# Expert blocks with both weight halves in one matmul, biases moved into the mixing, GRU state split shared with GpSimd

## The reference

```python
def step(h, xz):                              # 196 steps, h is (16, 192)
    h_z, h_r, h_n = jnp.split(h @ Wh.T + bh, 3, axis=-1)
    z = jax.nn.sigmoid(x_z + h_z)
    r = jax.nn.sigmoid(x_r + h_r)
    ncand = jnp.tanh(x_n + r * h_n)
    h_new = (1.0 - z) * ncand + z * h
...
top_v, top_i = jax.lax.top_k(softmax(xf @ gate_w.T), 2)     # the two best of 8, weights made to sum to 1
for e in range(8):
    w_e = jnp.sum(jnp.where(top_i == e, top_v, 0.0), axis=-1)
    y = _gelu(xf @ fc1_w[e].T + fc1_b[e]) @ fc2_w[e].T + fc2_b[e]      # 192 -> 512 -> 192
    out = out + w_e[:, None] * y
shared = _gelu(xf @ w1_w.T + w1_b) * (xf @ w3_w.T + w3_b) @ w2_w.T + w2_b
```

## Time and profile before

| | |
|---|---|
| median of 3 runs | 1919.51 us (1915.17 to 1924.06) |
| the profiled execution | 1919.37 us, span 1917.6 us |
| busy | PE 1503.1 (78%), PEld 1286.0 (67%), DVE 1313.1 (68%), ACT 951.3 (50%), POOL 740.5 (39%) |
| mean granted TensorE clock | 0.788 |
| GRU steps | 103.9 to 530.6 us of the span, PE 83% busy, clock 0.50 |
| expert blocks | 1241 to 1446 us, PE 100% busy, clock 0.99 |
| mixing | 1453 to 1486 us, PE 39% busy, clock 0.50 |

### The profile page before, as it was taken

The page is one execution under the profiler, slowest core; times in us unless marked ns, Lnnn a source line. Parts: engine busy times, 40 slices in busy tenths (PEclk is TensorE's granted clock), DMA queues, the critical chain, the costliest instruction groups (busy, mean ns, idle before and its releaser), DMA issues. The chain is left out here.

```text
span 1917.6 us, 51586 instructions
## 1 busy us (share of the span) xinstructions
PE 1503.1 (78%) x19477; PEld 1286.0 (67%) x19477; DVE 1313.1 (68%) x4844; ACT 951.3 (50%) x1918; POOL 740.5 (39%) x675
## 2 busy tenths in 40 slices
PE   4778888888845878889756899599994288888887
PEld 4667777777734867767544677388883277676766
DVE  7788888888857478778646674344444655787874
ACT  3633333333335577778614234344442256787881
POOL 3700000000022167779733012345550405686994
PEclk9955555555576999999885579799996589999998
DMA  2000000000032686668142204312224358676832
GB/s 82 4 4 4 4 4 4 4 4 4 4 106 87 164 232 147 147 126 148 26 127 74 90 25 162 117 57 66 63 63 147 103 156 225 140 165 127 161 59 58
DMA packets 62671, 167.20 MB, mean 87 GB/s; under 512 B 16648, under 2 KB 40184, under 8 KB 59740
## 3 DMA queue, kind: packets, MB, share of 16 engines
q1 hardware_dynamic: 57052, 151.05, 31.6%
q0 software_dynamic: 5376, 12.85, 2.3%
HBM read 95.84 MB, written 67.42 MB: 85 GB/s over the span
## 5 line engine op out<-in xcount | busy, mean ns | idle before, releaser
L903 POOL TENSOR_TENSOR l_arena<-l_arena,l_arena 98x784 fp32r<-98x784 f32 x192 | 354.7, 1860 | 110.0 <-PE l_ps L1012 72.5
L434 PE MATMUL gru_ps_r<-gru_hp,gru_wp 128*128 128x16 f16 x3920 | 200.5, 176 | 70.3 <-DVE gru_hp L406 69.5
L434 PEld LDWEIGHTS gru_ps_r<-gru_hp,gru_wp 128*128 128x128 f16 x3920 | 150.8, 105 | 92.0 <-DVE gru_hp L406 89.9
L842 POOL MEMSET l_arena<- 32x6272 f32 x2 | 10.6, 5319 | 511.3 <-POOLq L45 511.3
L1180 DVE TENSOR_REDUCE l_ps<-l_ps 98x4 f32<-98x784 f32 x192 | 187.5, 976 | 25.1 <-PE l_ps L973 20.2
L434 PE MATMUL gru_ps_n<-gru_hp,gru_wp 128*128 128x16 f16 x3920 | 191.2, 174 | 0.0
L1011 PE MATMUL l_ps<-l_arena,l_arena 128*66 128x196 f32 x768 | 163.1, 265 | 24.5 <-POOL l_arena L903 24.2
L489 ACT ACTIVATE gru_tr<-gru_ps_r,gru_unscale 128x32 f32<-128x32 f32 x196 | 56.4, 288 | 220.5 <-PE gru_ps_r L434 220.5
L1123 ACT ACTIVATE l_arena<-l_ps 98x784 fp32r<-98x784 f32 x192 | 158.4, 825 | 4.6
L1126 ACT ACTIVATE l_arena<-l_ps 98x784 f32<-98x784 f32 x192 | 157.0, 818 | 0.0
L1012 PE MATMUL l_ps<-l_arena,l_arena 128*66 128x196 f32 x768 | 156.3, 257 | 0.0
(11 more groups left out here) (344 smaller groups left out, 4642.7 us busy)
## 6 DMA issues: line engine op xcount, KB each, us to landing
l_arena<-qk SPq DMA_DIRECT2D x48, 588.0 KB
qk<-l_arena SPq DMA_DIRECT2D x48, 392.0 KB, 7.3
rel<-l_arena SPq DMA_DIRECT2D x24, 686.0 KB
l_arena<-rel SPq DMA_DIRECT2D x24, 686.0 KB
l_arena<-x SPq DMA_DIRECT2D x32, 294.0 KB, 6.4
qk<-l_arena SPq DMA_DIRECT2D x12, 784.0 KB, 14.4
l_arena<-in_experts_dram SPq DMA_DIRECT2D x8, 1152.0 KB, 7.5
l_arena<-picked SPq DMA_DIRECT2D x16, 294.0 KB
```

What stands on the lines that cost most here:

```text
L434: last = pe.matmul(out[:, b, B * m:B * m + B], wp[:, wi, g, m, :], hp[:, b, part, B * k:B * k + B], start=False, stop=True, skip_group_che ...
L903: pool.tensor_tensor(pl[:TH, g % 2, :, :], p32[:TH, g % 2, :, :], ph[:TH, g % 4, :, :].bitcast(f32), ALU.subtract).then_inc(pl_ready, 1)
```

## The change

It has three parts. In the GRU the gates are made by Sigmoid (`reset`, `keep`), `renew`, `new` and `held` (the whole old state) lie in PSUM, and GpSimd makes `kept` and its low part. In the expert blocks the low and high halves of a weight part go through TensorE side by side, as one matmul of 384 columns, and only the high half meets the low part of the hidden values; ScalarE copies the left half of the sum and VectorE adds the right one to it. The bias matmul is gone; instead `weigh_choices` makes a table of each token's 8 weights (three parts), which TensorE turns (`turn_gates`) and ScalarE copies (`keep_gates`), and in the mixing a matmul with 24 rows adds the weighted biases to each turned half. In order and loads: `xs` comes in eight pieces, each behind six more blocks; the last expert is loaded ahead of a store and split ahead of the first gather.

```diff
@@ gru, VectorE
-                    dve.scalar_tensor_tensor(rn[:, b, :], tr[:, b, :], 1.0, ps_n[:, b, :2 * B], ALU.add, ALU.mult).then_inc(rn_ready, 1)
+                    dve.tensor_tensor(rn[:, b, :], reset[:, b, :], ps_n[:, b, :2 * B], ALU.mult).then_inc(rn_ready, 1)
...
-                    dve.scalar_tensor_tensor(hp[:, 1 - b, KEPT_HIGH, :], tz[:, b, :], 1.0, half[:, b, :], ALU.add, ALU.mult).then_inc(kept_high, 1)
-                    dve.tensor_scalar(zc[:, b, :], tz[:, b, :], -0.5 * HSCALE, 0.5 * HSCALE, ALU.mult, ALU.add).then_inc(zc_ready, 1)
-                    dve.scalar_tensor_tensor(kept[:, b, :], tz[:, b, :], 1.0, half[:, b, :], ALU.add, ALU.mult).then_inc(kept_ready, 1)
+                    dve.tensor_tensor(hp[:, 1 - b, KEPT_HIGH, :], keep[:, b, :], held[:, b, :], ALU.mult).then_inc(kept_high, 1)
+                    dve.tensor_scalar(renew[:, b, :], keep[:, b, :], -HSCALE, HSCALE, ALU.mult, ALU.add).then_inc(renew_ready, 1)
...
-                    dve.tensor_tensor(hp[:, 1 - b, KEPT_LOW, :], kept[:, b, :], hp[:, 1 - b, KEPT_HIGH, :], ALU.subtract).then_inc(kept_low, 1)
...
-                    dve.tensor_scalar(two(half[:, 1 - b, :]), state[:, t + 1, :, :], 0.5, None, ALU.mult).then_inc(half_ready, 1)
+                    dve.tensor_tensor(held[:, 1 - b, :], new[:, b, :], kept[:, b, :], ALU.add).then_inc(held_ready, 1)
@@ gru, GpSimd
+                for t in range(T):
+                    b = t % 2
+                    pool.wait_ge(h_ready, t + 1)
+                    pool.wait_ge(keep_ready, t + 1)
+                    pool.tensor_tensor(two(kept[:, b, :]), two(keep[:, b, :]), state[:, t, :, :], ALU.mult).then_inc(kept_ready, 1)
+                    pool.wait_ge(kept_high, t + 2)
+                    pool.wait_ge(kept_ready, t + 1)
+                    pool.tensor_tensor(hp[:, 1 - b, KEPT_LOW, :], kept[:, b, :], hp[:, 1 - b, KEPT_HIGH, :], ALU.subtract).then_inc(kept_low, 1)
@@ gru, ScalarE
-                    act.activation(tr[:, b, :], ps_r[:, b, :2 * B], ACT.Tanh, scale=unscale[:, 0:1]).then_inc(tr_ready, 1)
+                    act.activation(reset[:, b, :], ps_r[:, b, :2 * B], ACT.Sigmoid, scale=unscale[:, 0:1]).then_inc(reset_ready, 1)
@@ mixture, SP
+                    if t == NT - 1:
+                        sp.wait_ge(summed3, 28)
+                        expert(7)
                     if t >= 1:
                         sp.wait_ge(y_ready, 2 * t)
...
-                sp.wait_ge(summed3, 28)
-                expert(7)
...
-                for k, (at, width) in enumerate(CHUNKS):
-                    sp.dma_start(xs[:width, k, :], y_dram[at:at + width, :]).then_inc(xs_in, 16)
+                for n in range(NT):
+                    sp.wait_ge(yg_ready, GATHERS * (n + 1))
+                    for k, (at, width) in enumerate(CHUNKS):
+                        cols = slice(n * TB, (n + 1) * TB)
+                        sp.dma_start(xs[:width, k, cols], y_dram[at:at + width, cols]).then_inc(xs_in, 16)
@@ mixture, GpSimd
+                for e in range(E - 1):
+                    split_tails(e)
                 pool.wait_ge(ids_ready, 2)
                 pool.wait_ge(summed3, 4 * NT)
                 pool.memset(bl[64:128, :, 128:256].bitcast(f32), 1.0 / 32).then_inc(tail_ready, 1)
+                split_tails(E - 1)
@@ mixture, TensorE, weigh
-                    pe.matmul(out, ones2[:, :], eb2[:, bass.ds(e, 1), :].rearrange("p a c -> p (a c)"), start=True, stop=False)
+                    def w(f):
+                        halves = experts[:, bass.ds(e, 1), LOW0:].rearrange("p a (h x) -> p (a h) x", h=2)
+                        return halves[:, :, F + f * C:F + (f + 1) * C]
+
                     for f in range(FB):
                         tok = slice(f * 128, (f + 1) * 128)
-                        pe.matmul(out, hgh[:, b % 2, tok], w(W2H, f), start=False, stop=False)
-                        pe.matmul(out, hgh[:, b % 2, tok], w(W2L, f), start=False, stop=False)
-                        last = pe.matmul(out, hgl[:, b % 2, tok], w(W2H, f), start=False, stop=f == FB - 1)
+                        pe.matmul(out, hgh[:, b % 2, tok], w(f), start=f == 0, stop=False, skip_group_check=True)
+                        last = pe.matmul(out[:, C:], hgl[:, b % 2, tok], w(f)[:, 1, :], start=False, stop=f == FB - 1, skip_group_check=True)
@@ mixture, TensorE, mixing
+                def turn_gates(n):
+                    if n >= 4:
+                        pe.wait_ge(gates_kept, n - 3)
+                    for j in range(GROUP):
+                        last = pe.transpose(ps[:3 * E, 4 + n % 4, j * TH:(j + 1) * TH], gates[:TH, n * GROUP + j, :], ident[:TH, :TH])
+                    last.then_inc(gates_turned, 1)
+
+                pe.wait_ge(gates_ready, 3)
+                pe.wait_ge(yg_ready, BLOCKS)
+                for n in range(2):
+                    turn_gates(n)
+                pe.wait_ge(bias_ready, 1)
                 for n in range(NT):
+                    if n + 2 < NT:
+                        turn_gates(n + 2)
                     for j in range(GROUP):
...
                         last.then_inc(y_turned, 1)
+                        pe.wait_ge(y_turned, i + 1)
+                        pe.wait_ge(gates_kept, n + 1)
+                        for k, (at, width) in enumerate(CHUNKS):
+                            out = ps[:width, 2 * (n % 2) + k, j * TH:(j + 1) * TH]
+                            last = pe.matmul(out, bias_parts[:, at:at + width], gate_cols[:3 * E, n % 4, j * TH:(j + 1) * TH],
+                                             start=False, stop=True, skip_group_check=True)
+                    last.then_inc(biased, 1)
@@ mixture, ScalarE
+                    if n >= 2:
+                        b = n - 2
+                        act.wait_ge(out_summed, b + 1)
+                        if b >= 2:
+                            act.wait_ge(yg_ready, b - 1)
+                        act.activation(yl[:, b % 2, :], ps_y[:, b % 2, :C], ACT.Copy).then_inc(yl_ready, 1)
+
+                def keep_gates(n):
+                    act.wait_ge(gates_turned, n + 1)
+                    if n >= 4:
+                        act.wait_ge(biased, n - 3)
+                    act.activation(gate_cols[:3 * E, n % 4, :], ps[:3 * E, 4 + n % 4, :TB], ACT.Copy).then_inc(gates_kept, 1)
+
+                keep_gates(0)
+                keep_gates(1)
                 for i in range(HALVES):
                     n, j = i // GROUP, i % GROUP
+                    if j == 0 and n + 2 < NT:
+                        keep_gates(n + 2)
@@ mixture, VectorE
+                def weigh_choices():
+                    dve.tensor_copy(bias_high[:, :], biases[:, :C]).then_inc(bias_rounded, 1)
+                    link(dve.tensor_tensor(share[:TH, :, :], pick1[:TH, :, :], over(w1), ALU.mult))
+                    link(dve.tensor_tensor(gates[:TH, :, 0:E], pick2[:TH, :, :], over(w2), ALU.mult))
...
-                        dve.tensor_copy(yg[:, b % OUTS, :], ps_y[:, b % 2, :]).then_inc(yg_ready, 1)
-
-                dve.wait_ge(xs_in, 32)
+                        dve.wait_ge(yl_ready, b + 1)
+                        dve.tensor_tensor(yg[:, b % OUTS, :], ps_y[:, b % 2, C:], yl[:, b % 2, :], ALU.add).then_inc(yg_ready, 1)
+
+                dve.wait_ge(xs_in, 32 * NT)
```

More of the change, by code:

```diff
@@ L322, in gru @@
         KEPT_HIGH, KEPT_LOW, NEW_HIGH, NEW_LOW, SUM_HIGH, SUM_LOW = range(6)
-        names = "tr tz zc rn cand n kept new half".split()
-        tr, tz, zc, rn, cand, tn, kept, new, half = (s.sb(n, [128, 2, 2 * B]) for n in names)
+        names = "reset keep rn cand n kept".split()
+        reset, keep, rn, cand, tn, kept = (s.sb(n, [128, 2, 2 * B]) for n in names)
         ps_r, ps_n, ps_z = s.ps("ps_r", 2), s.ps("ps_n", 2), s.ps("ps_z", 2)
+        shares = s.ps("shares", 1)[:, 0, :12 * B].rearrange("p (a b n) -> p a b n", a=3, b=2)
+        renew, new, held = (shares[:, a] for a in range(3))
         wo_raw = s.sb("wo_raw", [128, 2, CB, CP])
@@ L352, in _ @@
                 dve.memset(state[:, 0, :, :], 0.0).then_inc(h_ready, 1)
-                dve.memset(half[:, 0, :], 0.0).then_inc(half_ready, 1)
+                dve.memset(held[:, 0, :], 0.0).then_inc(held_ready, 1)
                 for part, ready in ((KEPT_HIGH, kept_high), (KEPT_LOW, kept_low), (NEW_HIGH, new_high), (NEW_LOW, new_low),
@@ L488, in _ @@
                     act.wait_ge(r_summed, t + 1)
-                    act.activation(tr[:, b, :], ps_r[:, b, :2 * B], ACT.Tanh, scale=unscale[:, 0:1]).then_inc(tr_ready, 1)
+                    act.activation(reset[:, b, :], ps_r[:, b, :2 * B], ACT.Sigmoid, scale=unscale[:, 0:1]).then_inc(reset_ready, 1)
                     act.wait_ge(z_summed, t + 1)
-                    act.activation(tz[:, b, :], ps_z[:, b, :2 * B], ACT.Tanh, scale=unscale[:, 0:1]).then_inc(tz_ready, 1)
+                    act.activation(keep[:, b, :], ps_z[:, b, :2 * B], ACT.Sigmoid, scale=unscale[:, 0:1]).then_inc(keep_ready, 1)
```

(14 more changed lines are left out.)

80 lines of the change are left out of this document (40 added, 40 removed).

## The result

The changed kernel took 1904.74 us (median of 8 runs, 1896.31 to 1908.39), the kernel before 1918.88 beside it (8 runs): ratio 0.991, interval 0.9885 to 0.9935. Forecast were 1886 and a gain of 33; the gain is 14. Timed once more, beside experiments 10 to 12 (experiment 9), the same kernel took 1893.13 for 1919.55, ratio 0.9848 (0.9818 to 0.9878): 26 less.

What follows compares the result with a forecast made beforehand. TensorE was taken to bound the expert blocks, latency the GRU loop, with room beside the mixing's loads. 0 - 37.5 + 2.5 - 17.5 - 0.5 + 20 = -33 gave 1886 us, range 1865 to 1907.

Steps and rivals of the forecast that it cites:

- GRU, forecast 0: GRU loop: Sigmoid, GpSimd's instructions and PSUM leave the 2.16 us step unchanged; sum 0, gain bounded at -17 us.
- the loop doesn't depend on VectorE's turn: GRU loop: the new high part waits for `n`, so taking `kept` off VectorE is worth nothing, at most 17 us.
- Halves and bias, forecast 0.67 a block: Expert blocks: 0.48 us from the removed bias matmul, 0.19 from halves side by side; -37.5 us for 56 blocks.
- The row buffer's loop, forecast +2.5: Expert blocks: shorter blocks leave gathers 0.54 us spare of 2.25; landings above 3.3 stall TensorE; +2.5 us, bounds 0 and +15.
- Blocks show waits for gathered rows: Expert blocks: a stated sign that the forecast is wrong; it expected 2.96 us blocks without a stall before the first 384-column matmul.
- rival C: Expert blocks: gathers become the bound, late by 0.3 in each block, +17 us, 1903 us in total; chance 0.08.
- Start of the blocks, forecast -17.5: Start of the blocks: earlier last expert and gathers bring the first transpose to 1221 from 1238.4; -17.5 us, bounds -18.5 and -10.
- the rule of the Trainium skill: GRU: two-input VectorE and GpSimd instructions on SBUF exclude each other; judged not to meet here; rival +49 us, chance 0.03.
- Choosing, forecast -0.5: Choosing: four large VectorE instructions go, eight small ones come, TensorE waits little on them; -0.5 us, bounds -3 and +2.
- Mixing, forecast +20: Mixing: added bias matmuls and the gates' order make a group 7.1 us for 4.1; +20 us, bounds +7 and +26.
- 1865 to 1907: Whole kernel: the total range in us, taking in the forecast and rivals A to D.
- the forecast's own 1875 to 1897: Whole kernel: the range in us of the main forecast of 1886, given a chance of 0.58.

Runs made afterwards that it cites:

- experiments 10 to 12: Changed kernel with gates ahead and bias in banks of its own (1875.2 us); that plus scatter one block later (1860.5); changed kernel with mixing input loaded whole (1893.77).
- experiment 9: The changed kernel measured again, unaltered, against the kernel before: 1893.13 us, ratio 0.9848.
- experiment 4: The kernel before with only the GRU's part of the change: 1915.6 us, ratio 0.9969.
- experiment 11: Changed kernel with gates ahead of the mixing, bias in banks of its own, and the scatter one block later: 1860.5 us, ratio 0.9684.
- experiment 6: The kernel before without the bias matmul of the expert blocks, leaving out the experts' second bias: 1901.21 us, one run.
- experiment 7: The kernel before with the halves side by side alone, bias matmul kept but moved to the block's end: 1906.9 us, one run.
- experiment 10: Changed kernel with all gates ahead of the mixing, a group's bias made by two matmuls in banks of its own, added apart by VectorE: 1875.2 us, ratio 0.976.
- experiment 12: Changed kernel with the input of the mixing loaded whole instead of in eight pieces: 1893.77 us, ratio 0.9862.
- experiment 1: Changed kernel with GpSimd's scatter of the blocks' sums one block later: 1898.5 us, ratio 0.9888.
- experiments 5 to 8: Changed kernel, sums written by SP (1873.93 us); kernel before without bias matmul (1901.21); kernel before, halves side by side (1906.9); changed kernel, three edits to scatter, gates, bias (1861.28).
- experiment 3: Changed kernel with the gates of all 8 groups turned and copied ahead of the mixing: 1896.35 us, ratio 0.9881.
- experiments 1 to 3: Changed kernel with the scatter one block later (1898.5 us), with expert numbers as constants (1896.18), with all gates ahead of the mixing (1896.35).

## Why the prediction was half right

*GRU, forecast 0, measured -5.3 in the steps and 4.9 in the time alone (experiment 4).* Sigmoid, GpSimd's two instructions and PSUM cost what I took. What failed is the sentence that the loop doesn't depend on VectorE's turn: it is true of a plain step, but I read one step of 2.16 where the mean of the 195 is 2.177. The two ends of the stretch, divided by its steps, would have shown it.

*Halves and bias, forecast 0.67 a block.* Right: the undisturbed block is 2.94 (experiment 11) for the forecast 2.96. The bias alone gives 0.46 to 0.48 for 0.48 (experiment 6). That leaves 0.21 for the halves, forecast 0.19; alone, with the bias matmul moved, they gave 0.26 (experiment 7).

*The row buffer's loop, forecast +2.5 with a bound of +15.* This is the term that was mis-sized. The stalls cost 13 us in experiment 9 (0.24 a block against experiment 11, times 55), and the lead of the gathers, one number, is worth 14.7 us of total time between experiments 10 and 11. The spare time itself came out as reckoned: from the landing of a block's rows to its transpose it is 2.29 us in the median before (forecast 2.25), 0.67 in experiment 9 (forecast 0.54), 3.37 in experiment 11. Two things were left out. I took the median landing, 2.8 us, and wrote that landings above 3.3 stall TensorE, but didn't count them: from the seventh block on, 11 of 50 took 3.34 to 4.21 in the kernel before, and 12 did in experiment 9. And a transpose that is late by a little also uncovers what is queued behind it, the load of the expert's number and the wait for `low`, some 0.7 us. An estimate from these: the 12 exceed 3.3 by 4.5 us together, and 0.7 for each of the eleven long waits ahead of `up` makes 7.7 more, 12 of the 13. The new loads of `xs` among the blocks, which I blamed, are not the cause: without them a block took 3.18 (experiment 12). "Blocks show waits for gathered rows" was one of my signs of being wrong, and it came true; the mechanism was rival C's, 17 us with a chance of 0.08.

*The late signals*, in no step and no rival: 12 us in the first measurement, nothing in the second. By them the measured gain is 14 and not 26. The block code of the kernel before doesn't meet them: experiment 4, on the chip of 1 to 3, has none. In it TensorE's signals fall due 0.72, 1.16, 2.95 and 3.17 us behind the start of a scatter's issue (medians). Of those due 2.1 to 2.9 us behind one, 22 of 29 were held in the changed kernel and 16 of 23 in experiment 1, so they may depend on where they fall against GpSimd's two issues; but of those due 0.6 to 0.9 behind one 8 of 29 were held too, and a held signal shifts GpSimd's next issue itself. The cause stays open: experiments 5 to 8, which were to tell it apart, ran on a chip where none was seen, and exclude neither the 384 columns nor the scatter, nor the recording of events.

*Start of the blocks, forecast -17.5, measured -15.6 and -16.0.* The size is right, the reason only half: experiment 12 shows that the pieces of `xs` add nothing to the early expert. Of the missing 1.5 us the profile shows the place: GpSimd's first tail takes 2.93 us beside VectorE's 1.47 of splitting (1210.86 and 1211.15 above). It took 1.43 with 0.30 of the splitting beside it in the earlier trace rows, and 1.28 to 1.30 with none for the third to seventh expert. That agrees with the rule of the Trainium skill (SBUF — State Buffer, "Who interferes with whom") that I had weighed for the GRU, where the two never met; I did not hold it against the expert that I moved next to VectorE's own half of it.

*Choosing, forecast -0.5.* Nothing to be seen: the shift against the kernel before is 3.4 us at the first rounding of an expert and 3.3 at each `finish` of the first seven tiles.

*Mixing, forecast +20, measured +18.0 and +18.3.* Right in mechanism and size: experiment 3 takes the order away and gets 11 back; experiment 10 also takes away most of a group's eight changes of rows, and gets 16.5 of experiment 9's 18.3 back.

The sum: -33 against -5.4 - 15.6 - 12.9 + 18.0 and +3.4 from stages that the change doesn't touch, -12.5 for the span's 12.6. That 1904.7 lies within 1865 to 1907 is in part luck. It lies outside the forecast's own 1875 to 1897 and next to rival C's 1903, but C's mechanism makes up only 13 us of it, the late signals 12, and the gain in the GRU that I had at nothing takes 5 back. In experiment 9, at 1893, the stalls and the GRU's gain partly cancel.

## What to carry to other kernels

When the engine that sets the pace gets faster, work out for every loop of buffers how far ahead its requests go, and if less than one of its steps is left, lengthen the lead before anything else: here one number was worth 15 us. A correction moved out of a busy stage into an idle one must not stand in the chain of the idle stage; made apart and ahead it cost 2 us for 18. Count the slow landings and not only the median one. And divide a stretch by its number of steps before you take one step for all.

## What the runs showed of the hardware

- TensorE's completion signals were recorded up to 2.4 us late in a stretch in which GpSimd issues indirect scatters and gathers: 54 of 206 in the changed kernel's first profile, 58 of 199, 42 of 186 and 48 of 203 in experiments 1 to 3, none of 224 in the changed kernel's second profile. TensorE goes on meanwhile; who waits for it doesn't. These four traces, and that of experiment 4 with no late signal, also lack 64 to 84 semaphore events, the other nine none.
- VectorE's list of 19 entries a step stalled at boundaries 128 entries apart, which made 28 steps 0.06 to 0.36 us longer, and a transfer of 8,192 bytes of instructions followed each of the 29 boundaries. With 16 entries a step no step was longer.
- GpSimd's 64 x 512 subtraction took 2.93 us while VectorE ran a 1.47 us subtraction with two inputs in SBUF, and 1.28 to 1.30 with none beside it.
- One matmul with two rows between matmuls with 128 cost 0.46 to 0.48 us a block (experiment 6).
- An indirect gather issued by GpSimd landed 2.8 us behind its issue in the median, but 11 of 50 took 3.34 to 4.21 us in the kernel before.
